# A graph kernel on one core: first tiles of four more columns through both hops early, column 0 finished early, seven more tiles without Sign in the first pass

## What is computed

```python
# layer 0
h = jnp.maximum(_layernorm(x), 0.0)
x1 = swish((adj @ h) @ W0 + b0)         # first hop
x  = x + swish((adj @ x1) @ W0 + b0)    # second hop
# layer 1
h = jnp.maximum(_layernorm(x), 0.0)
a = adj + eye; d = sum(a, axis=1) ** -0.5
out = x + ((a * d[:, None] * d[None, :]) @ h) @ W1.T + b1
```

## Time and profile before

| | us | how to read it |
|---|---|---|
| median of 3 runs | 1431.83 | 1430.1 to 1432.29 |
| the profiled execution | 1432.94 | its own time, 1.1 above the median |
| its span | 1431.1 | first to last instruction; granted clock 0.998 of 2.4 GHz in the mean |
| TensorE busy | 1380.6 | 6600 matmuls |
| VectorE busy | 1050.7 | 2325 instructions |
| ScalarE busy | 688.1 | 799 instructions |
| GpSimd busy | 59.3 | 47 instructions |
| loads of `adj` in the first pass | | 256 of 1 MB, 7.8 us from issue to landing in the median |
| loads of `adj` in the third pass | | 52 of 1 MB, 5.3 us from issue to landing in the median |

### The profile page before, as it was taken

One profiled execution on the slowest core, in us unless ns is written; L12 is line 12 of the kernel. 1 busy time (PEld: TensorE's weight loads), 2 busy tenths in 40 slices (PEclk: granted clock), 3 DMA queues, 4 the chain that ended last, 5 costly groups with the idle time before them and its releaser, 6 DMA issues.

```text
span 1431.1 us, 18441 instructions
## 1 busy us (share of the span) xinstructions
PE 1380.6 (96%) x6600; PEld 649.0 (45%) x6600; DVE 1050.7 (73%) x2325; ACT 688.1 (48%) x799; POOL 59.3 (4%) x47
## 2 busy tenths in 40 slices
PE   3789999999999999999999999999999999999997
PEld 1334444444444444444444454454444444444443
DVE  7778777899999988977684767786766566657630
ACT  6885647888777676567640122222422332233200
POOL 1100000000000010000000011100000000000000
PEclk9999999999999999999999999999999999999999
DMA  9999999999999988797740112112544534443300
GB/s 380 407 410 401 396 404 381 423 421 412 392 397 383 379 339 319 324 381 298 308 178 30 52 45 67 67 67 89 192 177 156 187 142 183 156 185 140 140 23 17
DMA packets 58419, 352.22 MB, mean 246 GB/s; under 512 B 6481, under 2 KB 6866, under 8 KB 18386
## 3 DMA queue, kind: packets, MB, share of 16 engines
q1 hardware_dynamic: 51696, 339.11, 60.0%
q10 hardware_dynamic: 6626, 11.87, 2.2%
HBM read 339.15 MB, written 11.80 MB: 245 GB/s over the span
## 4 chain that ended last, share of the span: by engine, by line
PE 76%; DMA 11%; DVE 5%; ACT 4%; issue 3%; DVEq 0%; SPq 0%; ACTq 0%
PE acc_ps L738 21%; PE acc_ps L737 21%; DMA ring<-adj 11%; PE acc_ps L672 8%; PE acc_ps L673 8%; PE early_ps L603 4%; PE early_ps L601 4%; PE z_ps L584 3%; PE kept_ps L611 2%; PE kept_ps L612 2%; ACT unused L897 1%; DVE marks L1062 1%; ACT node_b L833 1%; PE early_ps L642 1%; PE early_ps L641 1%
## 5 line engine op out<-in xcount | busy, mean ns | idle before, releaser
L897 ACT ACTIVATE unused<-ring 128x2048 uint8<-128x2048 uint32 x204 | 389.4, 1909 | 75.7 <-DMA ring<-adj 67.0
L672 PE MATMUL acc_ps<-marks,node_a 128*128 128x512 fp8e4 x960 | 366.5, 382 | 40.0 <-DVE node_a L1055 20.1
L738 PE MATMUL acc_ps<-ring,node_a 128*128 128x512 fp8e4 x1024 | 388.2, 379 | 0.0
L737 PE MATMUL acc_ps<-ring,node_a 128*128 128x512 fp8e4 x1024 | 388.1, 379 | 0.0
L673 PE MATMUL acc_ps<-marks,node_a 128*128 128x512 fp8e4 x960 | 366.5, 382 | 0.0
L1062 DVE TENSOR_SCALAR marks<-ring 128x2048 uint8<-128x2048 f32 x228 | 282.4, 1239 | 84.3 <-DMA ring<-adj 41.2
L1349 DVE TENSOR_SCALAR_CACHE_REDUCE count_a<-marks 128x2048 uint8<-128x2048 f32 x52 | 118.8, 2285 | 114.1 <-DMA marks<-adj 112.7
L434 DVE TENSOR_SCALAR ring<-bits 128x256 uint32<-128x256 uint32 (+1 forms) x784 | 159.1, 282 | 40.3 <-PE acc_ps L738 40.2
L672 PEld LDWEIGHTS acc_ps<-marks,node_a 128*128 128x128 f16 x960 | 94.2, 98 | 163.7 <-issue 55.9
L738 PE MATMUL acc_ps<-ring,node_b 128*128 128x512 fp8e5 x416 | 157.7, 379 | 0.0
L737 PE MATMUL acc_ps<-ring,node_b 128*128 128x512 fp8e4 x416 | 157.7, 379 | 0.0
(11 more groups left out here) (136 smaller groups left out, 1205.4 us busy)
## 6 DMA issues: line engine op xcount, KB each, us to landing
ring<-adj SPq DMA_DIRECT2D x256, 1024.0 KB, 7.8
marks<-adj SPq DMA_DIRECT2D x52, 1024.0 KB, 5.3
node_b<-x SPq DMA_DIRECT2D x4, 1024.0 KB, 11.3
xch<-x SPq DMA_DIRECT2D x16, 256.0 KB, 2.8
xn_scratch<-xnew ACTq DMA_DIRECT2D x16, 256.0 KB, 2.0
xch<-xn_scratch SPq DMA_DIRECT2D x16, 256.0 KB, 2.9
out<-xnew ACTq DMA_DIRECT2D x16, 256.0 KB, 2.0
part_scratch<-stage ACTq DMA_DIRECT2D x13, 256.0 KB, 7.1
```

The lines of the kernel that those rows point to most:

```text
L672: nc.tensor.matmul(acc_ps[c % 2][:, :], hi_of(node_a16, j), byte, start=(j == opens * TB), stop=False)
L737: nc.tensor.matmul(into[:, :], hi_of(node, j), byte.bitcast(E4), start=opens, stop=False)
L738: last = nc.tensor.matmul(into[:, :], lo_of(node, j), byte.bitcast(low), start=False, stop=closes)
L897: nc.scalar.activation(unused[:, :], loaded_slot(g).bitcast(U32), ACT.Sign, accum_out=nz_count[:, g:g + 1]).then_inc(counted, 1)
```

## The change

Four tables and the steps that read them are changed.

- `AHEAD` gets an entry behind tile 1.7: the first tile (one, not two) of columns 3, 4, 5 and 6 goes through both hops there. The pairs (13, 14), (11, 12) and (9, 10) stand behind tiles 3, 7 and 11 of column 2, and (7, 8) behind tile 7 of column 3. ScalarE's saves stand at other places accordingly, and VectorE separates the bits of the single tiles (`split_singles`) and joins them again when their column comes (`join_single`).
- Columns 0 and 1 are finished within tiles 0 to 3 of the next column. The eight kept blocks of node block 0 move from column 2 to tiles 8 to 15 of column 1.
- ScalarE marks six tiles of column 0 instead of eight; VectorE's list of steps in column 0 is written in another order; two one-element activations of ScalarE (`eps_root`) load the square-root table at the start and the sigmoid table at tile 0.13.
- The four single tiles and three more (1.0, 1.2 and 2.1) are not signed in the first pass. `LATE` has 59 tiles instead of 52, and `LATE_STEP` is 5 instead of 4.
- A mark also waits until the marks that it overwrites have been packed.

```diff
-ACT_MARKED = [1, 3, 4, 5, 7, 9, 11, 13] + [TC + i for i in range(1, TC, 2)] + [g for g in range(2 * TC, 5 * TC) if g % 4 == 3]
-AHEAD = {2 * TC + 7: (13, 14), 2 * TC + 11: (11, 12), 3 * TC + 7: (9, 10), 3 * TC + 11: (7, 8)}
+ACT_MARKED = [1, 3, 4, 7, 9, 11] + [TC + i for i in range(1, TC, 2)] + [g for g in range(2 * TC, 5 * TC) if g % 4 == 3]
+AHEAD = {TC + 7: (3, 4, 5, 6), 2 * TC + 3: (13, 14), 2 * TC + 7: (11, 12), 2 * TC + 11: (9, 10), 3 * TC + 7: (7, 8)}
+UNSIGNED = [TC, TC + 2, 2 * TC + 1]
+LATE = list(range(TC)) + UNSIGNED + [g for g in ACT_MARKED if g >= TC]
+LATE += [c * TC + i for i in range(2) for c in sorted(AHEAD_COLUMNS) if i < AHEAD_TILES[c]]
-LATE_STEP = 4
+LATE_STEP = 5
-FINISH_FIRST = {"sums out": 1, "project": 3, "bias": 5, "scale": 6, "sigmoid": 5, "gate": 7, "high": 7, "low": None}
+FINISH_FIRST = {"sums out": 0, "project": 0, "bias": 1, "scale": 1, "sigmoid": 1, "gate": 2, "high": 2, "low": 3}
-    return e.c >= 1 and e.i == (FINISH_FIRST if e.c == 2 else FINISH)[what]
+    return not e.ahead and e.c >= 1 and e.i == (FINISH_FIRST if e.c <= 2 else FINISH)[what]
+KEPT_SOURCE = {1: 0}
+KEPT_SOURCE.update((c, c - 2) for c in range(3, NC))
+FIRST_KEPT_AFTER = (8, 9, 10, 11, 12, 13, 14, 15)
...
             act.wait_ge(eps_set, 1)
+            nc.scalar.activation(eps_root[:, :], eps_col[:, :], ACT.Sqrt)
             root(0)
...
                 if e.at >= MARK_RING:
                     dve.wait_ge(tile_mm, multiplied_upto(e.at - MARK_RING))
+                    dve.wait_ge(pack4_ready, (e.at - MARK_RING) // GT + 1)
...
+            def split_singles(r, c):
+                dve.wait_ge(bits_ready, r + 1)
+                link = chain(dve, single_step, 0)
+                link(nc.vector.tensor_scalar(bits_v[:, c + 2:c + 5:2, 1, :], bits_v[:, c + 1:c + 4:2, 1, :], 0x55555555, None,
+                                             ALU.bitwise_and))
+                link(nc.vector.tensor_scalar(bits_v[:, c + 1:c + 4:2, 1, :], bits_v[:, c + 1:c + 4:2, 1, :], 1, 0x55555555,
+                                             ALU.logical_shift_right, ALU.bitwise_and))
...
             first_spread(1)
             h_low(0)
+            mark(ORDER[2])
             first_scales(1)
...
-                done = 0
-                for of in (nz_count[:, 0:TC], nz_count[:, TC:2 * TC].rearrange("p (i s) -> p i s", s=2)[:, :, 1],
+                for k, first, step, n in late_runs():
+                    of = nz_count[:, first:first + step * (n - 1) + 1:step]
+                    link(nc.vector.tensor_tensor(differ[:, NC + k:NC + k + n], of, late_one[:, k:k + n], ALU.not_equal))
```

More of the change, by code:

```diff
@@ L62, with late_runs @@
 COUNT_STEPS = 11
-ACT_MARKED = [1, 3, 4, 5, 7, 9, 11, 13] + [TC + i for i in range(1, TC, 2)] + [g for g in range(2 * TC, 5 * TC) if g % 4 == 3]
-AHEAD = {2 * TC + 7: (13, 14), 2 * TC + 11: (11, 12), 3 * TC + 7: (9, 10), 3 * TC + 11: (7, 8)}
-AHEAD_COLUMNS = [c for pair in AHEAD.values() for c in pair]
-FIRST_AHEAD = min(AHEAD_COLUMNS)
-LATE = list(range(TC)) + [g for g in ACT_MARKED if g >= TC] + [c * TC + i for c in sorted(AHEAD_COLUMNS) for i in range(2)]
-LATE_STEP = 4
+ACT_MARKED = [1, 3, 4, 7, 9, 11] + [TC + i for i in range(1, TC, 2)] + [g for g in range(2 * TC, 5 * TC) if g % 4 == 3]
+AHEAD = {TC + 7: (3, 4, 5, 6), 2 * TC + 3: (13, 14), 2 * TC + 7: (11, 12), 2 * TC + 11: (9, 10), 3 * TC + 7: (7, 8)}
+AHEAD_COLUMNS = [c for ahead in AHEAD.values() for c in ahead]
+AHEAD_TILES = {c: 4 // len(ahead) for ahead in AHEAD.values() for c in ahead}
+SINGLES = [c for c in AHEAD_COLUMNS if AHEAD_TILES[c] == 1]
+PAIRED = [c for c in AHEAD_COLUMNS if AHEAD_TILES[c] == 2]
+FIRST_AHEAD = min(AHEAD_COLUMNS)
+UNSIGNED = [TC, TC + 2, 2 * TC + 1]
+LATE = list(range(TC)) + UNSIGNED + [g for g in ACT_MARKED if g >= TC]
+LATE += [c * TC + i for i in range(2) for c in sorted(AHEAD_COLUMNS) if i < AHEAD_TILES[c]]
+LATE_STEP = 5
+def late_runs():
+    runs, k = [], 0
+    while k < len(LATE):
+        n = min(2, len(LATE) - k)
+        step = LATE[k + 1] - LATE[k] if n == 2 else 1
+        if step <= 0:
+            n, step = 1, 1
+        while n > 1 and k + n < len(LATE) and LATE[k + n] - LATE[k + n - 1] == step:
+            n += 1
+        runs.append((k, LATE[k], step, n))
+        k += n
+    return runs
 class Entry:
@@ L80, in __init__ @@
         self.c, self.i = g // TC, g % TC
-        self.hole = not ahead and self.c in AHEAD_COLUMNS and self.i < 2
+        self.hole = not ahead and self.i < AHEAD_TILES.get(self.c, 0)
 def entries():
@@ L88, in entries @@
         for c in AHEAD.get(g, ()):
-            for i in range(2):
+            for i in range(AHEAD_TILES[c]):
                 order.append(Entry(len(order), c * TC + i, True))
@@ L615, in _, with take_ahead @@
             pe.wait_ge(w_in, 32)
-            def unit_ahead(now, pair, c, at):
+            def take_ahead(now, before, c, at):
                 into = acc_ps[(now + 1) % 2]
+                tiles = range(AHEAD_TILES[c])
                 pe.wait_ge(nT_ready, now)
-                if pair > 0:
-                    pe.wait_ge(x_saved, pair)
-                for i in range(2):
+                if before > 0:
+                    pe.wait_ge(x_saved, before)
+                for i in tiles:
                     pe.wait_ge(marked, marked_upto(at + i))
@@ L628, in unit_ahead @@
                         nc.tensor.matmul(into[:, :], hi_of(node_a16, j), byte, start=(j == 0), stop=False)
-                        last = nc.tensor.matmul(into[:, :], lo_of(node_a16, j), byte, start=False, stop=(j == 2 * TB - 1))
+                        last = nc.tensor.matmul(into[:, :], lo_of(node_a16, j), byte, start=False, stop=(j == len(tiles) * TB - 1))
                 last.then_inc(x_done, 1)
-                if pair > 0:
-                    pe.wait_ge(y_saved, pair)
+                if before > 0:
+                    pe.wait_ge(y_saved, before)
                 if now >= KEPT:
                     pe.wait_ge(early_ready, now - KEPT + 1)
-                for i in range(2):
+                for i in tiles:
                     pe.wait_ge(node_ready, i + 1)
@@ L874, in _ @@
                     c, i, g = e.c, e.i, e.g
-                    if g == 5:
-                        root(2)
                     if e.ahead:
-                        first, second = AHEAD[OWN_BEFORE[e.at]]
-                        if (c, i) == (second, 1):
-                            save_x(first)
-                            save_y(first)
+                        ahead = AHEAD[OWN_BEFORE[e.at]]
+                        which = ahead.index(c)
+                        if which > 0 and i == AHEAD_TILES[c] - 1:
+                            save_x(ahead[which - 1])
+                            if which < 3:
+                                save_y(ahead[which - 1])
                         continue
@@ L1083, in pack_last @@
                 p2 = pack2.rearrange("p (g h w) -> p g h w", g=GB, h=2)
-                if e.ahead:
+                if e.ahead and e.c in SINGLES:
+                    to = bits_v[:, e.c + 1:e.c + 4:2, 1, :]
+                elif e.ahead:
                     pair = sorted((e.c, ORDER[r * GT + 2].c))
@@ L1220, in _ @@
             h_low(4)
-            mark(ORDER[8])
+            mark(ORDER[10])
             pack_half(1)
```

110 lines of the change are left out of this document (61 added, 49 removed).

## The result

| | before | after |
|---|---|---|
| median of 4 runs, us | 1431.22 (1430.1 to 1432.29) | **1439.17** (1438.83 to 1440.25) |
| profiled execution, its time / span | 1432.94 / 1431.1 | 1439.45 / 1437.6 |

What follows compares the result with a forecast made beforehand. Taken as the bound: arrival of the tiles just ahead of column 8 and VectorE's work after it. 1432.9 - 2.0 + 3.9 = 1434.8, or 1433.7 us against the median, 1.9 us longer; range 1428.8 to 1438.0.

Steps and rivals of the forecast that it cites:

- Third part: Third pass, first late step: the fifth unsigned tile's load and count make TensorE wait 3.9 us once, bounds 3 and 7.
- a rival of 0.30: Third pass: the wait on the fourth piece leaves TensorE at its lower clock, 1.7 us more, 1436.4 us; chance 0.30.
- Fill: Columns 3 to 6 and moved pairs: 11.9 us idle between 60 and 120 us reappear at 185 to 390; worth 0.
- TensorE was waiting for it: Reason for the 0: tile 2 of column 8 is still the 143rd tile loaded, and TensorE waited for it.
- Second part: Loads ahead of column 8: tiles arrive 2.0 us earlier, bounds -1 and 3.
- Sum: 2.0 us earlier: Arrivals ahead of column 8: 1.3 (start) + 1.5 (column 4) - 0.8 (late loads in column 2) = 2.0 us.
- Its two gains: Arrivals: 1.3 us at the start, bounds 0 and 1.5, and 1.5 us at column 4, bounds 0 and 1.5.
- the stall at column 4: Column 4: a load issued late because ScalarE's save waited for TensorE; the stall goes, 1.5 us, bounds 0 and 1.5.
- Taken as nothing: VectorE, 120 to 387 us: two extra short instructions per single column and the extra wait on every mark cost nothing.
- priced at 0.8 with 2 as its bound: Tiles 0 to 3 of column 2: column 1's finishing steps delay marks, signs and loads; 0.8 us, bounds 0 and 2.
- The three tiles that lose their Sign: Said to lie where column 1's finish delays loads, and to keep that loss small, at 0.8 us.
- the arrivals pay: Rival: the late count in the third pass is hidden and only the earlier arrivals count, 1429.3 us; chance 0.12.

Runs made afterwards that it cites:

- e2_before_five: The kernel before with LATE_STEP 5 instead of 4 alone (52 late tiles in 11 steps): 1436.52 us, 5.3 us more than before, ratio 1.004.
- experiment 2: The kernel before with only the change's steps of the first 16 tiles (square-root table first, six ScalarE marks, VectorE's new order): 1431.60 us, ratio 1.000.

## Why the prediction was wrong

**Third part: right, its clock undervalued.** One wait was forecast at 3.9 us and came at 3.65, in the step and behind the instruction named; the later steps did not wait. The sum took the clock at full speed and left 1.7 us to a rival of 0.30. It happened, at 1.4 us. The argument against it, that TensorE comes out of a full pass, did not hold.

**Fill: right as a sum, its condition narrower than it said.** The idle time moved as described (5.9 us gone, 7.5 us come back). "TensorE was waiting for it" rested on 0.93 us at column 8 in one trace; in other executions of the same first pass (`e2_before_five`) TensorE does not wait there. So loads and TensorE were nearly level before, and earlier loads alone brought nothing (experiment 2). With VectorE relieved the changed kernel was 2.0 us faster than the kernel before; that the fill is what brought it is likely, not shown.

**Second part: this step failed.** "Sum: 2.0 us earlier" came out as 1.4 us later in the trace and 3.3 us longer in the medians. (Its terms, each at its bound, give -2 to 3, not "-1 and 3".) Its two gains were there, 2.5 us at the start for 1.3 and the stall at column 4 gone (3.5 us of loads for 1.5); the first is given back between 60 and 120 us (2.4 us), as it is with the start alone, and why is open. What was lost besides was larger:

- 3.8 us of loads between 280 and 360 us. The sentence that failed is "Taken as nothing: ... since VectorE stands idle for 16% of the time from 120 to 387 us". The average hid 80 us in which VectorE had under 3 us to spare, and the sum counted two short instructions and left out GpSimd's eight additions, at each of which an instruction of VectorE is 0.41 to 1.07 us longer. Taking them out won 4.35 us, giving smaller ones to the kernel before cost it 2.0.
- 2.1 us between 120 and 160 us, priced at 0.8 with 2 as its bound. "The three tiles that lose their Sign ... are what keeps it small" is not borne out: signed again, they cost nothing. And in the kernel without singles the loss goes with the moved pairs, not with the early finish of column 1, where the prediction had put it.

One slip has no part in the result: the rival "the arrivals pay" subtracts 2.5 us for a second part that was summed at 2.0.

The account in medians: the fifth late tile 4.6 us (5.3 by itself in the kernel before), the first pass 3.3 us, together 7.95. Against the first pass's 3.3, GpSimd's additions stand for 2 (smaller ones, given to the kernel before) to 4.35 (taken out of the changed one), and with them cut and four late tiles first the change is 1.3 us faster than before (1430.21 for 1431.55). The gain at the start brings nothing that can be measured by itself (experiment 2). How the losses in columns 0 to 2 divide between the finish, the saves and the pairs in the full change is open.

## What to carry to other kernels

List every instruction that a change issues, on the engines that look idle too: eight additions on an engine with 5% load cost 2 to 4 us, since they take turns with the engine that sets the pace. Judge spare time in the stretch where the work lands, not over the phase. And a batch that "only" grows from four to five should be priced with the slot that its last item has to wait for, and with the clock behind the wait; here it was enough to leave the first batch at four. Before a difference of 1 to 2 us between two traces is read as an effect, look at a second trace of unchanged code: here the same load lay 1.8 us apart in two.

## What the runs showed of the hardware

- GpSimd's additions and most of VectorE's instructions exclude each other for whole instructions: an addition of 128x512 float32 took 1.27 us at 239.39 us and 2.31 us behind a mark under way, and VectorE's next work took 1.07 us more (2.47 for 1.40 us). Unpackings, marks, packing steps (2.29 us for 1.22 at 333.70 us) and counts were all made longer; the addition of the bias, with one operand from PSUM, was not (0.68 us). Beside an addition from 316.48 to 318.13 us a mark took 2.17 us for 1.23, in the kernel after:

```profile
316.31 0.69 DVE L1166 TENSOR_SCALAR count_a<-bits 128x1024 uint32<-128x1024 uint32 x1
317.04 2.17 DVE L1105 TENSOR_SCALAR marks<-ring 128x2048 uint8<-128x2048 f32 x1
```

- TensorE came out of 3.87 us between two starts at its lower clock for seven matmuls, although it had been busy for 614.6 of the 615 us from 401 to 1016 us, and out of 2.44 us at full clock.
